# The first batch's second-unit maxima are carried ahead of the late rows, in a fused FFN, attention, FFN kernel

## What is computed

```python
x = x + 0.5 * ffn(layernorm(x))          # x: 4 x 1024 x 128, f32
x = x + attn(layernorm(x), w_qkv, w_proj)
x = x + 0.5 * ffn(layernorm(x))

def attn(x, w_qkv, w_proj):              # 16 heads of 8 columns
    q, k, v = split_heads(x @ w_qkv)
    att = einsum('bhnd,bhmd->bhnm', q, k) * 8 ** -0.5 + slopes * arange(N)
    att = softmax(where(causal, att, big_neg))
    return (att @ v) @ w_proj
```

## Time and profile before

| | us |
|---|---|
| median of 3 runs | 1018.42 (1017.79 to 1022.6) |
| profiled execution, its own time | 1019.16 |
| its span in the profile | 1017.4 |
| PE busy | 913.8 |
| DVE busy | 657.3 |
| ACT busy | 508.5 |
| POOL busy | 394.3 |

### The profile page before, as it was taken

One profiled execution on the slowest core, in us unless ns is written; L12 is line 12 of the kernel. 1 busy time (PEld: TensorE's weight loads), 2 busy tenths in 40 slices (PEclk: granted clock), 3 DMA queues, 4 the chain that ended last, 5 costly groups with the idle time before them and its releaser, 6 DMA issues.

```text
span 1017.4 us, 19580 instructions
## 1 busy us (share of the span) xinstructions
PE 913.8 (90%) x6961; PEld 569.1 (56%) x6961; DVE 657.3 (65%) x1680; ACT 508.5 (50%) x824; POOL 394.3 (39%) x463
## 2 busy tenths in 40 slices
PE   3596989878897999999999999999999888969996
PEld 3475989655333444544444544445453347969864
DVE  5763335527886678887788787887868646324422
ACT  1142656422254566656656565565566654636532
POOL 6667545554650410002201005006510373665564
PEclk9787999989597999999999999999999996979999
DMA  9612546355110132400421201314000012536432
GB/s 302 214 54 85 174 134 169 93 163 119 42 38 15 55 79 49 96 3 1 130 51 39 58 3 55 97 31 96 4 3 1 26 50 88 173 115 169 128 84 67
DMA packets 84260, 85.36 MB, mean 84 GB/s; under 512 B 11732, under 2 KB 73444, under 8 KB 81700
## 3 DMA queue, kind: packets, MB, share of 16 engines
q1 hardware_dynamic: 50842, 55.08, 20.7%
q0 software_dynamic: 8192, 16.79, 5.9%
q10 hardware_dynamic: 25132, 12.26, 4.1%
HBM read 52.48 MB, written 37.45 MB: 88 GB/s over the span
## 4 chain that ended last, share of the span: by engine, by line
PE 54%; DMA 17%; DVE 11%; issue 7%; POOL 4%; ACT 2%; DVEq 2%; POOLq 2%; SPq 0%
PE banks L1895 10%; PE banks L1865 9%; PE banks L1878 9%; DMA region_c<-sorted_y,pos 9%; PE banks L1784 6%; PE banks L1796 5%; DMA region_b<-sorted_y,pos 4%; DVE nmax L1447 3%; PE banks L1881 2%; PE banks L1868 2%; ACT work L1055 2%; PE banks L1772 2%; DMA m_scr<-mp 1%; DVE nmax_late_keys L1447 1%; PE banks L1661 1%
## 5 line engine op out<-in xcount | busy, mean ns | idle before, releaser
L1055 ACT ACTIVATE work<-banks 128x1024 f32<-128x1024 f32 (+3 forms) x384 | 300.6, 812 | 219.2 <-PE banks L1881 166.6
L1447 DVE TENSOR_REDUCE nmax<-banks 128x1 f32<-128x512 f32 (+3 forms) x432 | 271.5, 665 | 62.3 <-PE banks L1868 34.6
L1865 PE MATMUL banks<-ks,qs 75*128 75x512 bf16 (+3 forms) x576 | 178.7, 341 | 12.6 <-DVE nmax L1447 5.2
L1878 PE MATMUL banks<-qs,ks 78*128 78x512 bf16 (+3 forms) x576 | 156.1, 333 | 9.1 <-DMA qs<-m_scr 5.9
L1895 PE MATMUL banks<-work,vaug 128*9 128x512 f32 (+3 forms) x1536 | 163.5, 498 | 0.0
L801 POOL DMA_INDIRECT sorted_x<-region_b,pos x112 | 111.9, 999 | 118.6 <-DVEq L1276 63.0
L1334 DVE COPY region_c<-w 128x512 f32 x184 | 73.4, 440 | 114.2 <-PE banks L1796 105.4
L1447 DVE TENSOR_REDUCE nmax_late_keys<-banks 128x1 f32<-128x384 f32 (+3 forms) x176 | 109.4, 637 | 42.7 <-PE banks L1868 38.2
L1865 PEld LDWEIGHTS banks<-ks,qs 75*128 75x128 bf16 x576 | 56.0, 100 | 132.5 <-DVE nmax L1447 66.5
L1784 PE MATMUL banks<-xTp,region_c 128*128 128x128 f32 x736 | 104.4, 288 | 2.6 <-ACT xTp L952 2.4
L1881 PE MATMUL banks<-identb,maskb 128*128 128x128 bf16 x512 | 104.0, 223 | 0.0
(11 more groups left out here) (203 smaller groups left out, 1178.8 us busy)
## 6 DMA issues: line engine op xcount, KB each, us to landing
xld<-sorted_x SPq DMA_DIRECT2D x92, 128.0 KB
sorted_y<-ysb ACTq DMA_DIRECT2D x92, 128.0 KB
qs<-q_scr SPq DMA_DIRECT2D x36, 192.0 KB
ks<-k_scr SPq DMA_DIRECT2D x36, 192.0 KB
q_scr<-qp SPq DMA_DIRECT2D x15, 256.0 KB
region_c<-q_scr SPq DMA_DIRECT2D x12, 192.0 KB
region_c<-k_scr SPq DMA_DIRECT2D x12, 192.0 KB
k_scr<-kp SPq DMA_DIRECT2D x9, 256.0 KB
```

What stands on the lines that cost most here:

```text
L1055: nc.scalar.activation(pT[s % 2][pair][:, :, 0:w], ps_s[pair][:, :, 0:w], ACT.Exp).then_inc(s_e, 1)
L1447: nc.vector.tensor_reduce(dst, ps_in_turn[SLOT["bank", u * NB + n]][:, 0:len(pieces) * w].rearrange("p (h j) -> p h j", j=w), axis=AXX, op ...
L1865: last = mm(dst, qs[g][0:PASS1_ROWS, h, it * P:(it + 1) * P], ks[g][0:PASS1_ROWS, h, j0:j0 + w], start=True, stop=not diagonal)
L1878: last = mm(ps_s[pair][:, j, 0:w], ks[g][:, h, jt * P:(jt + 1) * P], qs[g][:, h, i0:i0 + w], start=True, stop=not diagonal)
```

## The change

SyncE's `max_rows(0, 1)` is issued directly after `max_rows(0, 0)`, ahead of the waits for the first FFN's adds and ahead of the late rows' DMAs. In the loop over batches it is left out of the first iteration, and the loop is a Python one, so that its three iterations stand one after another in SyncE's program. The other engines' programs stay as they are.

```diff
                 load_rows(g)
             max_rows(0, 0)
+            max_rows(0, 1)
 
             sp.wait_ge(ffn[0].add, BLOCKS + DVE_PARTS // TOP_K)
             sp.wait_ge(s_padd, 1)
...
             bias_rows(UNITS - 1)
             load_rows(UNITS - 1)
-            with sp.Fori(0, BATCH - 1) as b:
-                max_rows(b, 1)
+            for b in range(BATCH - 1):
+                if b:
+                    max_rows(b, 1)
                 max_rows(b, 2)
                 write_parts(b + 1)
                 rows_of(b + 1, 0, b)
```

## The result

| | before | changed |
|---|---|---|
| median of 17 runs each, us | 1017.79 | 1011.38 |
| profiled execution, its span | 1017.4 | 1012.4 |

The ratio is 0.9931, with a 95% interval of 0.9908 to 0.9954: by the ratio it is faster by 7.0 us, between 4.7 and 9.4; the medians are 6.4 apart. The forecast was 8.6 us and 1009.8.

What follows compares the result with a forecast made beforehand. Bound at the first FFN/attention seam: unit 1's maxima write queued behind late-row loads, stalling TensorE. Wait 5.6 plus half-speed stretch 3.0 gave 8.6 us, late rows and loop 0: 1018.42 - 8.6 = 1009.8 us, range 1007.4 to 1013.0.

Steps and rivals of the forecast that it cites:

- Part 1: First FFN/attention seam: unit 1's maxima go first, ending TensorE's wait (5.6 us) and the half-speed stretch (3.0), gain 8.6 us.
- excess of 8.6 to 8.9: Distance between maxima of units 1 and 2, 45.52 us, over the second and third batches' 36.93 and 36.59.
- The write's 1.45 us: Unit 1's maxima write at the seam: predicted time from issue to landing, taken from the write before unit 5.
- slack of 0.65 to 0.9 us: Before unit 1's scores: maxima rows arrive this much before TensorE wants them at 305.23, so its wait goes altogether.
- nine DMAs: SyncE's queue at the seam: issued ahead of the maxima's write, six being 192 KB loads, blamed for its 7.07 us landing.
- The rule of the clock: Half-speed stretch after the seam: skill's rule charges 4.5 us for 9 us, total 10.1; forecast used 3.0, total 8.6.
- Rival C: Half-speed time after the seam gives back its full half: gain 10.1 us, time 1008.3; chance 0.06.
- Parts 2 and 3: Late rows go second at no cost, margin 19 us; the written-out batch loop gains 0, within 0.3 us either side.
- Rival D: Seam: write stays slow at 7.07 us, or the read becomes so; 1017.6 or 1017.2, no change; chance 0.09.
- rival E: Late rows become the bound, landing 33 us later than worked out, making the kernel slower, 1023.5; chance 0.03.
- Rival B: Behind the attention, shifted clock stretches give back 3.5 us: gain 5.1, time 1013.3 or a little better; chance 0.14.

Runs made afterwards that it cites:

- e5: Changed kernel with the six loads back ahead of the write, issued 3.8 us before unit 1's last maxima; 1020.66 us, ratio to before 1.0040.
- e6: The changed kernel unedited, run again on a second chip; 1012.65 us, ratio to before 0.9947, maxima of units 1 and 2 36.60 us apart.
- e1: Kernel before with only the batch loop written out, order of DMAs kept; ratio to before 1.0029 (0.9975 to 1.0082).
- e4: ScalarE instead of SyncE issues write and read of unit 1's maxima, late rows as before, lag free; maxima of units 1 and 2 43.32 us apart.
- e9: The kernel before, unedited, profiled a second time; maxima of units 1 and 2 36.59 us apart, no stall.
- e10: e4 with the wait of e5: ScalarE issues write and read, six loads ahead, lag held; write 7.2 us, maxima of units 1 and 2 45.96 us apart.
- e12: Changed kernel with three tile-to-tile DMAs replacing the maxima's write and read in all units; ratio to before 0.9966 (0.9915 to 1.0018).
- e7: As e5, but only two of the six loads ahead of the maxima's write; write 3.1 us, maxima of units 1 and 2 36.98 us apart.
- e8: As e5, but four of the six loads ahead of the maxima's write; write 5.6 us, maxima of units 1 and 2 42.40 us apart.
- e11: Changed kernel with 30 spare 192 KB copies between the maxima's read and the six late loads; TensorE waited 6.0 us, maxima of units 1 and 2 43.15 us apart.

## Why the prediction was right, and where its size was off

**Part 1, the mechanism, held.** The stall and its half-speed stretch went together, SyncE's write went out at the lag of 0.03 us, and TensorE started unit 1 as in the second batch, 4.47 us behind the start of the maxima's last part against 4.46 there. The distance that followed, 36.60, is the third batch's 36.59 and not the second's 36.93. The excess of 8.6 to 8.9 was there, 8.92 between the two profiles and 9.2 between e5 and e6. The write's 1.45 us, taken from unit 5, was too low: the read went out 1.94 us behind it here and 1.74 in e6. With 1.81 to 2.05 for the read, of the slack of 0.65 to 0.9 us some 0.2 to 0.4 was left, which was enough.

**The term that was mis-sized is that same 8.6, taken as what every execution loses.** It came from a single profile with a lag of 3.8 us from SyncE's wait, 3.9 from the last add. The landing of the write follows the last load's issue and not its own: from the end of that issue to the read's issue it was 7.3 us in the earlier trace rows, 7.3 in e1, 7.0 in e4 and e9, 7.6 in e5 and 7.4 in e10, though the write went out between 0.04 and 4.95 us behind it. (In e9, with the 4.95, a write with nothing ahead would have landed as late.) In the first profile that issue ended 0.6 us behind the maxima, and TensorE was 5.6 us late. Each us that the issue ends earlier takes one us off the lateness, and once it ends some 5 us ahead of the maxima nothing is left: in e1 it was 4.3 us ahead, with a wait of under 1 us and a distance of 36.59. The lag from the end of the last add to the maxima lies ahead of all that the edits touch (but for e12, which also carries unit 0's maxima otherwise), so every profile shows a natural one. Where the kernel before takes 1018 us it was 3.9 (the first profile), 4.9 (e6), 5.1 (e5), 7.5 (e7, e8) and 7.7 us (changed); on the two slower chips it lay between 6.4 and 10.0.

In the order of before, an estimate from these rows gives TensorE's lateness. The last issue ends 4.5 us after the last add (301.66 - 297.12), the write is down 7.3 later, the rows are there 1.8 after that, and TensorE wants them 4.2 after the maxima's end. So it is late by 9.4 us less the lag. That makes 5.5 for the first profile (5.6 measured), 2.8 for e4 with its lag of 6.6 (2.9), nothing for e1 with 9.4 (0.7, where one of the loads' issues took 1.01 us instead of 0.36) and for e9 with 10.0 (nothing). For the changed kernel's 7.7 it makes 1.7.

The first profile had the smallest lag of the fourteen, and so, by this estimate, the largest loss of the order of before. For the six lags above, the lateness runs from 1.7 to 5.5, and with the costs measured in e4, e7, e8 and the first profile as bounds the mean loss is an estimated 3.6 to 7.8 us. The measured 7.0 us, and 5.4 between the medians of before and e6, fit that. That 8.6 came as near to 7.0 as it did was in part luck: it holds for one lag. That the lag sets the loss is shown for profiles; that the spread of lags makes the medians what they are is only argued, as most timed executions have no trace here.

**Where the loss sat.** I put it in the queue, behind nine DMAs. e10 shows that the order within a queue is not it: six loads in flight hold up a write of 24 KB on another queue as long. The Trainium skill ("DMA: Bandwidth & Descriptors", section "Issuing engines are not separate DMA queues") says that DMAs of all issuers run on the same 16 engines and interleave. That a second queue gave no escape, 7.2 us against 7.6, agrees; but the write was not mixed in among the loads all along, as the 4 us without one of its packets show (e10). The Trainium skill (the same page, section "Queues, rings and completion order") adds that a completion count lands only after every earlier write from that DMA engine, across its queues. That would make the semaphore late even where the data is not. It is not what held e10 up: three quarters of the write's own packets are recorded only from 317.5 on, and the read went out 0.7 us after the last of them. Why they came so late stays open.

**The rule of the clock.** The rule of the Trainium skill ("TensorE: Matmul & The Clock Gate", section "HAM oscillation — how this bites in real kernels") had 4.5 us for 9 us at half speed, the rows 3.0. e5 gave 3.2 for 10.2 us at half speed (a clock of 0.70 on the mean of 315 to 332), where the rule makes an estimated 5.1, and e8 2.5 for 6.9 us, where it makes an estimated 3.4. The rows were the better guide. VectorE's 10.73 of 11.00 us in 309 to 320 fit the reason given, that it takes over when TensorE is fast again; no run tests that by itself. Rival C falls: its 10.1 us stand against 9.2 between e5 and e6.

**Parts 2 and 3** held: no wait for the late rows, 18 us in hand against 19 (e11), and nothing from the loop (e1). Rival D fell with the first profile, and rival E with e11. Rival B, a gain partly given back behind the attention, did not show: the time from unit 15's maxima to the end was 223.0 before and 218.4 after, and it lies between 219.8 and 222.0 in e5 to e8, whose seams differ by up to 9 us. The stretch between units 14 and 15 that cost the changed profile 4.8 us is not there in e6. What makes the clock fall there in some executions, in the changed profile with TensorE busy before and after, stays open.

## What to carry to other kernels

A small DMA on the critical path should be issued before bulk loads that can wait, and here it did not help to give it a queue of its own. Find the slack of the bulk loads first: here 18 us.

When a stall hangs on two engines that reach a point independently, one profile shows one lag between them. Ask for the lag, work out the loss as a function of it, and forecast the gain over the lags that occur. An added wait that holds the lag makes such a loss measurable.

## What was not expected of the hardware

Six loads of 192 KB delay a 24 KB write on another engine's queue by as much as one on their own: 7.2 against 7.6 us. Two and four such loads on its own queue made it 3.1 and 5.6.

TensorE's 1.1 us of lateness at full speed cost 0.4 us, while 3.3 us of lateness, after which the clock stood at 1.2 GHz for a while (0.77 on the mean of 15 us), cost 5.8.

In the changed profile the clock fell to 1.2 GHz between units 14 and 15 although TensorE had been busy for 11.00 of 11.00 us (744 to 755, at a clock of 1.00), and this cost 4.8 us; in e6 the same program did not show it.

Two chips of three ran the kernel before at a median of 1065 to 1066 us, the other at 1018. In the profiles the difference lies outside the attention: from unit 15's maxima to the end it is 247 to 262 us on the slower ones and 218 to 223 on the other, while most distances within the attention agree to hundredths. The exceptions are the seam, and those from unit 7 to 8, 12 to 13 and 14 to 15.
